# Expert outputs scaled per tile and added into DRAM by an accumulating indirect DMA, in place of a gather and sum at the end

## The reference

```python
x = x + xattn(layernorm(x), ctx, ctx)      # 16 heads, 1601 context rows for each sequence
x = x + ssm(layernorm(x))                  # a state-space scan over the 64 positions
x = x + ffn(layernorm(x))
# ffn: shared expert plus the 2 best of 12 experts, by softmaxed router logits
ys = geglu(xf @ Ws1 + bs1) @ Ws2 + bs2
top_val, top_idx = top_k((xf @ Wr + br) / 1.5, 2)
w = one_hot(top_idx) weighted with softmax(top_val)
yE = geglu(xf @ We1[e] + be1[e]) @ We2[e] + be2[e]     # every expert e
yr = sum over e of yE[e] * w[:, e]
return ys + yr
```

## Time and profile before

| | |
|---|---|
| median of 3 runs | 1607.47 us (1606.13 to 1611.21) |
| the profiled execution, its own time | 1613.23 us |
| its span | 1611.5 us |
| mean granted TensorE clock | 0.967 of full speed |
| busy share PE, PEld, DVE, ACT, POOL | 85%, 64%, 83%, 65%, 62% |
| moved by DMA | 132.85 MB, mean 82 GB/s |

### The profile page before, as it was taken

The page is one execution under the profiler, slowest core; times in us unless marked ns, Lnnn a source line. Parts: engine busy times, 40 slices in busy tenths (PEclk is TensorE's granted clock), DMA queues, the critical chain, the costliest instruction groups (busy, mean ns, idle before and its releaser), DMA issues. The chain is left out here.

```text
span 1611.5 us, 33493 instructions
## 1 busy us (share of the span) xinstructions
PE 1366.9 (85%) x12636; PEld 1032.0 (64%) x12636; DVE 1342.2 (83%) x1692; ACT 1055.0 (65%) x2454; POOL 995.4 (62%) x820
## 2 busy tenths in 40 slices
PE   5899999999999999969667676767676699999992
PEld 4788888887888888756233333333333588888882
DVE  4899999999999999975699999999999434666662
ACT  3666666666666665526599899899898134555550
POOL 1778888888888788637367666667676032323323
PEclk9899999999999999998799999999999889999996
DMA  4611111111111110015560200300000016888872
GB/s 120 187 42 36 45 39 43 41 44 36 49 36 43 42 43 22 1 21 140 147 116 15 40 6 1 45 1 1 1 1 1 1 50 252 307 310 301 311 272 87
DMA packets 104155, 132.85 MB, mean 82 GB/s; under 512 B 39515, under 2 KB 95266, under 8 KB 100553
## 3 DMA queue, kind: packets, MB, share of 16 engines
q1 hardware_dynamic: 91496, 59.85, 15.0%
q0 software_dynamic: 9312, 67.90, 11.8%
q10 hardware_dynamic: 3200, 3.15, 0.6%
HBM read 110.44 MB, written 14.45 MB: 77 GB/s over the span
## 5 line engine op out<-in xcount | busy, mean ns | idle before, releaser
L555 POOL TENSOR_TENSOR half<-prob 128x512 f32<-128x512 f32 (+1 forms) x208 | 266.7, 1282 | 110.6 <-ACT prob L591 109.0
L587 ACT ACTIVATE prob<-ps_s,mx 128x64 f32<-128x64 f32 (+1 forms) x624 | 151.5, 322 | 237.4 <-DVE prob L700 237.4
L1346 DVE TENSOR_TENSOR state<-ps_u,state 128x1024 f32<-128x1024 f32 x252 | 296.9, 1219 | 4.3
L695 DVE TENSOR_REDUCE mx<-ps_s 128x16 f32<-128x1024 f32 (+1 forms) x208 | 253.3, 1218 | 13.1 <-PE ps_s L628 9.4
L1305 PE MATMUL ps_y<-state,cz 128*32 128x256 f32 x2048 | 247.8, 384 | 2.1 <-DVE state L1346 1.1
L1229 ACT ACTIVATE ps_a<-A,dt 128x256 f32<-128x256 f32 x504 | 210.4, 463 | 39.1 <-DVE state L1341 39.1
L628 PE MATMUL ps_s<-qbd,kT 64*128 64x256 f32 (+1 forms) x1664 | 217.4, 396 | 21.6 <-ACT prob L587 16.0
L700 DVE TENSOR_TENSOR prob<-ps_s,mx 128x832 f32<-128x832 f32 (+1 forms) x208 | 213.1, 1024 | 7.1
L1213 POOL TENSOR_TENSOR state<-direct,state 128x1024 f32<-128x1024 f32 x64 | 151.5, 2368 | 89.1 <-PE ps_y L1305 89.1
L1287 PE MATMUL ps_u<-x_rows,b_diag 48*128 48x256 bf16 x1024 | 79.4, 275 | 146.7 <-DVE state L1346 134.2
L628 PEld LDWEIGHTS ps_s<-qbd,kT 64*128 64x128 f32 (+1 forms) x1664 | 150.9, 184 | 66.0 <-issue 34.7
(11 more groups left out here) (243 smaller groups left out, 3136.3 us busy)
## 6 DMA issues: line engine op xcount, KB each, us to landing
raw<-in_ctxT_dram SPq DMA_DIRECT2D x80, 268.0 KB, 2.8
x_rows<-ssm_x SPq DMA_DIRECT2D x96, 64.0 KB
raw<-in_ctxT_dram SPq DMA_DIRECT2D x16, 261.0 KB, 2.7
b_diag<-zeros SPq DMA_DIRECT2D x2, 2048.0 KB, 9.0
x_slots<-zeros SPq DMA_DIRECT2D x1, 3456.0 KB, 13.5
xg<-x_slots SPq DMA_DIRECT2D x27, 128.0 KB, 6.1
y_slots<-y SPq DMA_DIRECT2D x27, 128.0 KB, 5.0
ssm_x<-xp ACTq DMA_DIRECT2D x8, 384.0 KB, 5.1
```

What stands on the lines that cost most here:

```text
L555: pool.tensor_tensor(half[0:rows, :, :], prob[0:rows, g % SLOTS, :, 0:L // 2], prob[0:rows, g % SLOTS, :, L // 2:L], ALU.add).then_inc(hal ...
L695: nc.vector.tensor_reduce(mx[0:rows, g % 2, :], part, AX_X, ALU.max, negate=True)\
L1346: nc.vector.tensor_tensor(h, flat(ps_u[k % 2][:, :, :]), h, ALU.add).then_inc(state_ready, 1)
```

## The change

Each slot row now has 258 columns: the 256 of x, the token's number (an integer), and the token's share (weight) of this expert. Slots that no pair fills carry a number from 1024 up, one for each partition, and the share zero; the zero fill is now two DMAs, one of 256 columns and one of the 2 last (8 bytes in each of 3456 rows). The rows are scattered from a buffer `f["rows"]` that holds each row twice, once for each of its two experts. Before its per-tile loop SP stores x with the shared expert's result into a DRAM buffer `sums`. For each routed tile SP loads the two extra columns (`info`), DVE scales the result by the share as it copies it from PSUM, and POOL adds the tile into `sums` by an indirect DMA with addition. Each such DMA waits for the one before. The store to `y_slots` in the loop, the gathers, the sums on DVE and the eight output stores are gone; one DMA copies `sums` to the output, DRAM to DRAM.

```diff
-                    sp.dma_start(d["x_slots"].rearrange("(t p) d -> p t d", p=P),
-                                 sb["zeros"][:, :].unsqueeze(1).broadcast_to([P, RTILES, D])).then_inc(slots_cleared, 16)
+                    slots = d["slot_rows"].rearrange("(t p) d -> p t d", p=P)
+                    sp.dma_start(slots[:, :, 0:D], sb["zeros"][:, :].unsqueeze(1).broadcast_to([P, RTILES, D]))\
+                        .then_inc(slots_cleared, 16)
+                    sp.wait_ge(ones_ready, 2)
+                    sp.dma_start(slots[:, :, D:D + 2], sb["unused"][:, :].unsqueeze(1).broadcast_to([P, RTILES, 2]))\
+                        .then_inc(slots_cleared, 16)
...
+            c.link(pool.memset(sb["unused"][:, :], 0.0))
+            c.link(pool.iota(sb["unused"][:, 0:1].bitcast(U32), pattern=[[0, 1]], base=TOK, channel_multiplier=1,
+                             allow_small_or_imprecise_dtypes=True))
...
         @block.sync
+            def load_info(T, turn, b):
+
+                if not known(turn, 1):
+                    sp.wait_ge(added[b], turn * 16)
+                sp.dma_start(info[b][:, :], slot_rows(T)[:, D:D + 2]).then_inc(info_loaded[b], 16)
 
             def one(kind, T, turn, b):
                 if not (isinstance(turn, int) and turn == RTILES // BUFS - 1):
                     load_x(T + BUFS, turn + 1, b)
-                sp.wait_ge(y_taken, T + 1)
-                sp.dma_start(d["y_slots"][bass.ds((T - TT) * P, P), :], y[b][:, :]).then_inc(y_stored[b], 16)
-
+                    load_info(T + BUFS, turn + 1, b)
+
+            def set_sums(t):
+                sp.wait_ge(y_taken, t + 1)
+                sp.dma_start(d["sums"][t * P:(t + 1) * P, :], sb["x"][:, t, :]).then_inc(sums_set, 16)
+
+            sp.dma_start(d["sums"][TOK:TOK + P, :], sb["zeros"][:, :]).then_inc(sums_set, 16)
+            for t in range(TT - 3):
+                set_sums(t)
             sp.wait_ge(scattered, 16 * 2 * TT)
             for b in range(BUFS):
                 load_x(TT + b, 0, b)
+                load_info(TT + b, 0, b)
+            for t in range(TT - 3, TT):
+                set_sums(t)
             all_tiles(sp, one, routed_only=True)
-            for t in range(TT):
-                sp.wait_ge(out_ready, t + 1)
-                sp.dma_start(d["out"][t * P:(t + 1) * P, :], sb["x"][:, t, :]).then_inc(stored, 16)
-            sp.wait_ge(stored, 16 * TT)
+            for b in range(BUFS):
+                sp.wait_ge(added[b], 16 * RTILES // BUFS)
+            sp.dma_start(d["out"].rearrange("(p t) d -> p (t d)", p=P),
+                         d["sums"][0:TOK, :].rearrange("(p t) d -> p (t d)", p=P)).then_inc(stored, 16)
+            sp.wait_ge(stored, 16)
 
         @block.gpsimd
+            def add(i):
+
+                if i == 0:
+                    pool.wait_ge(sums_set, 16 * (TT + 1))
+                else:
+                    pool.wait_ge(added[(i - 1) % BUFS], 16 * ((i - 1) // BUFS + 1))
+                pool.wait_ge(y_taken, TT + i + 1)
+                pool.indirect_dma_start(d["sums"][:, :],
+                                        bass.IndirectOffsetOnAxis(ap=info[i % BUFS][:, 0:1].bitcast(U32), axis=0),
+                                        y[i % BUFS][:, :], None, compute_op=ALU.add).then_inc(added[i % BUFS], 16)
+
+            for i in range(2):
+                pool.iota(f["rows"][:, :, i, D:D + 1].bitcast(U32), pattern=[[P, TT], [0, 1]], base=0, channel_multiplier=1,
+                          allow_small_or_imprecise_dtypes=True).then_inc(rows_made, 1)
+            pool.tensor_copy(f["rows"][:, :, 1, 0:D], f["xln"]).then_inc(rows_made, 1)
...
             for i in range(RTILES):
...
+                if i >= BUFS:
+                    add(i - BUFS)
+            for i in range(RTILES - BUFS, RTILES):
+                add(i)
...
     take_y (DVE):
-                        dve.wait_ge(y_stored[b], turn * 16)
-                    nc.vector.tensor_copy(y[b][:, :], ps_y[:, 0:D]).then_inc(y_taken, 1)
+                        dve.wait_ge(added[b], turn * 16)
+                    dve.wait_ge(info_loaded[b], (turn + 1) * 16)
+                    nc.vector.tensor_scalar(y[b][:, :], ps_y[:, 0:D], info[b][:, 1:2], None, ALU.mult).then_inc(y_taken, 1)
```

More of the change, by code:

```diff
@@ L660, in outputs @@
                 ins.then_inc(pv_done, 1)
-            pe.wait_ge(ones_ready, 4)
+            pe.wait_ge(ones_ready, 6)
             pe.wait_ge(bv_chain, 9)
@@ L1509, in experts @@
         den = sbuf("den", [P, TT])
-        share = sbuf("share", [P, TT, 2])
+        share = [f["rows"][:, :, i, D + 1] for i in range(2)]
         pick = sbuf("pick", [P, TT, 2, E])
@@ L1539, in experts @@
         hidT = sbuf("hidT", [P, 2, HR // 2])
-        back = sbuf("back", [P, TT, 2, D])
+        info = [sbuf(f"info_{b}", [P, 2]) for b in range(BUFS)]
         ps_a = [ctx.enter_context(nc.psum_tensor(f"e_ps_a{i}", [P, 512], F32)) for i in range(2)]
@@ L1555, in experts @@
         x_loaded = [sem(f"e_x_loaded{b}") for b in range(BUFS)]
-        y_stored = [sem(f"e_y_stored{b}") for b in range(BUFS)]
-        y_back = [sem(f"e_y_back{t}") for t in range(TT)]
+        info_loaded = [sem(f"e_info_loaded{b}") for b in range(BUFS)]
+        added = [sem(f"e_added{b}") for b in range(BUFS)]
+        rows_made, sums_set = sem("e_rows_made"), sem("e_sums_set")
         x_turned, xTh_ready, xT_ready = sem("e_x_turned"), sem("e_xTh_ready"), sem("e_xT_ready")
@@ L1561, in experts @@
         hid_done, hid_turned, hidT_ready = sem("e_hid_done"), sem("e_hid_turned"), sem("e_hidT_ready")
-        down_done, y_taken, out_ready = sem("e_down_done"), sem("e_y_taken"), sem("e_out_ready")
+        down_done, y_taken = sem("e_down_done"), sem("e_y_taken")
         stored = sem("e_stored")
@@ L1613, in _, with slot_rows @@
         def _(sp):
+            def slot_rows(T):
+                return d["slot_rows"][bass.ds((T - TT) * P, P), :]
             def load_x(T, turn, b):
@@ L1617, in load_x @@
                     sp.wait_ge(x_turned, T - TT - BUFS + 1)
-                sp.dma_start(xg[b][:, :], d["x_slots"][bass.ds((T - TT) * P, P), :]).then_inc(x_loaded[b], 16)
+                sp.dma_start(xg[b][:, :], slot_rows(T)[:, 0:D]).then_inc(x_loaded[b], 16)
+            def load_info(T, turn, b):
+                if not known(turn, 1):
+                    sp.wait_ge(added[b], turn * 16)
+                sp.dma_start(info[b][:, :], slot_rows(T)[:, D:D + 2]).then_inc(info_loaded[b], 16)
             def one(kind, T, turn, b):
@@ L1641, in _ @@
                     j = 2 * t + i
-                    pool.indirect_dma_start(d["x_slots"][:, :],
+                    pool.indirect_dma_start(d["slot_rows"][:, :],
                                             bass.IndirectOffsetOnAxis(ap=slot[:, j:j + 1], axis=0),
-                                            f["xln"][:, t, :], None).then_inc(scattered, 16)
+                                            f["rows"][:, t, i, :], None).then_inc(scattered, 16)
             pool.wait_ge(owner_ready, 1)
@@ L1851, in weigh @@
                 c.link(nc.vector.tensor_scalar(den[:, :], ex[:, :], 1.0, None, ALU.add))
-                c.link(nc.vector.reciprocal(share[:, :, 0], den[:, :]))
-                c.link(nc.vector.tensor_tensor(share[:, :, 1], ex[:, :], share[:, :, 0], ALU.mult))
+                c.link(nc.vector.reciprocal(share[0], den[:, :]))
+                c.link(nc.vector.tensor_tensor(share[1], ex[:, :], share[0], ALU.mult))
             def assign_tiles():
@@ L1941, in tail @@
                 take_y("routed", TT + RTILES - 1, RTILES // BUFS - 1, BUFS - 1)
[L1942 to L1952, removed]
             choose()
@@ L1965, in perceiver_layer @@
               "gmask": sbuf("gmask", [P, HG]),
-              "minus_half": sbuf("minus_half", [P, TT]), "zeros": sbuf("zeros", [P, D])}
+              "minus_half": sbuf("minus_half", [P, TT]), "zeros": sbuf("zeros", [P, D]), "unused": sbuf("unused", [P, 2])}
+        d["slot_rows"] = nc.dram_tensor("slot_rows", (RTILES * P, D + 2), F32, kind="Internal").ap()
+        d["sums"] = d["y_slots"][0:TOK + P, :]
         slots_cleared = ctx.enter_context(nc.semaphore("slots_cleared"))
@@ L2014, in perceiver_layer @@
                 ssm_output(nc, sb, m)
-            f["xln"] = m["wzx"][:, :, :].rearrange("p k n -> p (k n)").rearrange("p (t d) -> p t d", t=TT)
+            f["rows"] = sbuf("rows", [P, TT, 2, D + 2], to=ssm)
+            f["xln"] = f["rows"][:, :, 0, 0:D]
             layer_norm(nc, sb, "ln3", f["xln"])
```

3 lines of the change are left out of this document (2 added, 1 removed).

## The result

The changed kernel took 1640.39 us (median of 4 runs, 1628.54 to 1643.06), the kernel before 1608.4 us: a ratio of 1.0174, with a 95% interval of 1.0148 to 1.0201. It is slower, by some 20 to 32 us.

The account below looks back on a forecast made before the run. The prediction took PE to bound the kernel, at 8.56 us a tile. End -16.6, loop +30, first x +3.3 and slot fill +6 made +22.7 us on 1607.5, so 1630, with a range of 1604 to 1672.

Parts of the forecast that it names:

- The ring: Routed tiles' loop: x loads wait on SP behind info for the add, and the delay returns every two tiles; +30 us.
- E: In the loop, how late x lands for PE: 2.5 us, paid 12 times, once for each two tiles.
- the delay covered: In the loop, w1 goes out 1.25 us later, but behind w2, which is still being moved: no cost.
- The clock: In the loop, PE at half clock after long stalls, about 2.5 us lost in attention; part of the growing-stalls rival, 0.23.
- The rival of the growing stalls: In the loop, longer x delays or half clock after each stall: 60 us, in all +53, 1660; chance 0.23.
- The first x: Start of the routed tiles: stores of sums ahead on SP make the first x late for PE; +3.3 us.
- The slot fill: Attention: 3456 pieces of 8 bytes delay the load of raw, for which ACT already waits; +6 us.
- The end: After the last y: the gathers go, the last add and the 1 MB copy remain; -16.6 us.
- At nothing: No cost from POOL's copy of 2048 columns, DVE's scaling copy, the earlier info load, or w1 going out later.
- the end wins: Rival: in the loop x is not late, E is 0, so the end decides: -7 us, 1600; chance 0.11.
- nearly even: Rival: E between 0.2 and 1.0, loop 2 to 12 us, whole within 5 us of nothing; chance 0.08.

Follow-up runs that it names:

- a0: The changed kernel itself, run again on chip 3: 1630.54 us against 1610.38 for the kernel before, ratio 1.0123.
- e3: The changed kernel with the five stores of sums moved behind the first x loads: 1646.43 us, ratio 1.0104 to the kernel before.
- e2: The changed kernel with the fill of the two extra columns moved to the state-space stage: 1638.57 us, ratio 1.0065 to the kernel before.
- e1: The changed kernel with info loaded one tile later on SP: 1619.8 us against 1628.24 for the kernel before, ratio 0.9952.
- e4: The kernel before, with the x load of tile T+4 waiting for the y store of tile T: 1638.56 us against 1628.24, ratio 1.0061.
- e9: e6 with info loaded two tiles later instead of one and w1 issued ahead of the add: 1586.94 us, ratio 0.9866 to the kernel before.
- e8: The changed kernel with slot rows of 1280 bytes (320 columns instead of 258): 1635.16 us, ratio 1.0152 to the kernel before.
- e5: The changed kernel with the indirect DMA writing rows instead of adding them: 1624.45 us, ratio 1.0099 to the kernel before.
- e6: The changed kernel with info one tile later, sums stores behind the first x loads, both slot fills in the state-space stage: 1590.35 us, ratio 0.9862 to before.
- e7: e6 with w1 of tile T+4 issued ahead of the add of tile T on POOL: 1599.82 us, ratio 0.9922 to the kernel before.

## Why the prediction was right, step by step

The forecast was 1630 us, +22.7, with a range of 1604 to 1672; measured were 1640.4 at the result and 1630.5 in a0. The mechanism of the loop was right; that its sum came out at +30 is in part luck, as shown next.

*The ring, +30.* Right in mechanism. w2 was taken at 6.0 us to landing and took 5.9 in the tile shown; the add at 0.7 behind it, 0.8; from info to the landing of x 6.1, 7.1. E was taken at 2.5 us, 12 times; PE's waits of 30.8 us in the loop are 12 times 2.6. But they fell on 20 tiles, not on every second one, and two of them, 4.8 and about 4 us, are of another size than the rest and are counted below. Where no such stall fell, two tiles took 18.1 to 20.6 us from y to y instead of 17.0. In e3, where no wait was longer than 2.3 us and the clock stayed at its full level all through, the loop's stretch is 22.8 us above 195.8, 12 times 1.9, and in e2 24.5. The ring by itself is worth that: an E of 1.9 or 2.0, not 2.5. e1 shows the cause by taking it away; e4 shows that a late release of x alone costs time. What was not foreseen is the issue of the add, 2.36 us where the prediction's 1.25 from issue to issue had been that of a load, which sends w1 out 2.8 us later than before. The prediction called the delay covered; e1 leaves 3 us in the loop, e9 takes 2 of them out, and in the changed kernel the stalls for x hid it.

*The clock.* The rival of the growing stalls had a second mechanism in it, PE at half clock after a long wait, and it took place twice, not at each stall. The longest wait of the loop, 4.8 us at 1532 us, and one of about 4 at 1576 were followed by this (PE, PEld, DVE, ACT, POOL busy, granted clock, DMA share, GB/s):

```profile
1534.00:1538.00 4.00, 1.22 (x6) 1.16 (x7) 0.00 (x0) 0.00 (x0) 0.97 (x1) 0.74 0.94 250
1538.00:1542.00 4.00, 4.00 (x13) 3.28 (x12) 2.12 (x2) 2.12 (x3) 0.00 (x0) 0.50 0.70 278
...
1576.00:1580.00 4.00, 0.33 (x3) 0.25 (x3) 0.57 (x2) 0.00 (x0) 2.48 (x2) 1.00 0.96 256
1580.00:1584.00 4.00, 4.00 (x16) 3.19 (x15) 1.58 (x2) 2.12 (x3) 0.00 (x0) 0.57 0.85 316
```

That is the low level, 1.2 GHz (or a mix of both in 0.57), after a stretch in which PE did little. From y to y these two tiles took 16.2 and 14.0 us and the one next to each 8.4, so the pairs took 24.6 and 22.4 where the others took some 19.2: 8 to 9 us more, an estimate from these rows. a0 had one such stall (4.4 us) and e8 one (5.0), both with the clock at 0.50 behind them; e2, e3 and e5 had none. What made them long isn't shown. So the +32.4 of this profile are some 24 of the ring and some 8 of this rival, and the forecast's +30 hit the sum of both. The other stalls of this profile, of up to about 2 us, left the clock at its full level. At 2.3 and 2.4 us it went either way: behind one such wait each in a0, e2 and e5 the clock fell, to 0.50 to 0.53, behind one in e3 it did not.

*The first x, +3.3.* PE waited 3.2 us for it and 4.0 were lost at the result, 2.9 in a0. e6, with the stores behind, has them back.

*The slot fill, +6.* Right in size in most profiles, too small in that of the result. From ACT's first copy of raw to its last the kernel before took 622.2 and 622.3 us (e4), the changed one 628.4 to 629.6 in a0, e1, e3 and e5, 6 to 7 us more, and 633.2 in the profile of the result, 11 more, where ACT's wait rose by 11.4. That only 8.2 of the 11 are left at the first load of w need not be an effect of the fill, since the stretches between vary by as much from profile to profile. The small pieces were priced at 20 ns for each of 216, 4.3 us, and the small fill lands 4.3 us behind the zeros (81.6 and 77.3); e2 confirms it with 4 to 5. Mis-sized was the zero fill itself: "adds a little", 1.7 us, became 5.1 in this profile and 2.8 to 3.9 in the others that have it in attention.

*The end, -16.6.* -16.9 in the table, but by errors that cancel. From the last y to the end 13.0 us were forecast and 11.2 measured, a gain of 18.3. The last add landed after 3.7 us (3.4 taken) and the copy after 5.8 (6.5 taken); the wait for the add before, 1.2 us in all, had been excluded; and from the landing of the copy to the end it is 0.4 us, where 2.5 had been carried over from the kernel before. The stretch from w2 of tile 26 to the last y, 21.9 instead of 20.5 us, takes 1.5 back.

*At nothing.* POOL's copy of 2048 columns is indeed not seen: from the last product of state space to the first scatter there are 58.3 us where it was 59.9.

*The rivals.* That the add lands so soon that the end wins did not happen: the Trainium skill's fit (DMA: Bandwidth & Descriptors, Anatomy of one DMA — SWDGE (gpsimd) path) gives an estimated 3.8 us for w2, the trace 5.9, with other traffic beside it. With 3.8 and the forecast's other terms x would land at 1461.6, an estimate too, and E would be 0.3: so even by that fit x would not be on time, though the prediction says so, and the case would have been "nearly even". e1 shows what the case of E at 0 would have been worth on its chip: 0.5% faster than before.

## What to carry to other kernels

An engine that issues DMAs in program order, as SP does here, turns each wait into a wait for everything behind it. Before adding one, list what is queued behind it and how much time each of those has to spare; here a load of 1 KB that nobody needed for two tiles held up the one that PE needed next, and the cure was to ask for it one tile later, not to make the add faster. Where the late item feeds the thing that releases it, count how many tiles the ring has: a delay is paid again for each turn. And before a term is judged by one pair of profiles, look how much the same stretch differs between kernels that are alike there: here up to 8 us before the first load of w. A gain at the end of 17 us was real, and became a gain of the kernel only when the waits that came with it had been moved.

## What the runs showed of the hardware that I had not expected

The issue of an indirect DMA with addition, 128 rows of 1 KB, kept POOL for 1.56 us on an idle queue and 2.36 in the median of the loop; the plain one took 0.96 and 1.75. It landed after 3.7 and 2.4 us on an idle queue.

SP was held for 6.6 to 7.6 us by the issue of one DMA of 3456 pieces of 8 bytes in attention and for 11.8 to 13.1 us in the state-space stage (e6, e7, e9), with the zero fill of 3456 KB just ahead of it; without that fill ahead (e2) the same issue took 0.40 us.

On chip 15 all four kernels paused in the shared tiles, while the first six loads of w ran. In e4 ACT shows it, and the stage from 1335 to 1340 us:

```profile
1337.34 0.38 ACT L1782 ACTIVATE gel<-e_ps_g 128x256 f32<-128x256 f32 x1 [10.92 <-remote]
```
```profile
1335.00:1340.00 5.00, 0.00 (x0) 0.00 (x0) 0.00 (x0) 0.38 (x1) 1.88 (x2) 0.50 1.02 418
```

PE did nothing, the profile names no semaphore for it, and the DMA engines were full. In the kernel before, on the other chips, the same loads ran beside a busy PE. The 18 us that are lost there are about what the kernel before takes longer on this chip (1628.24 against 1608 to 1610). The profile names no instruction as the releaser. That the engines waited for their next instructions (the page of the profile counts queues of kind "instruction", 147 packets in the kernel before) is only a guess, and why this chip alone has the pause stays open.
